# A graph stack on one core: the adjacency cast inside the loads that GpSimd issues, the other loads held back behind its pieces

## The chip, the cores and the metric

The kernel runs on one core of a Trainium2 chip. The metric is the device time of one execution in microseconds (us), and lower is better. The kernel before was timed three times; the median is 681.71 us, the runs lie between 681.45 and 682.27 us.

## What is computed

Four graph layers follow each other on the same 2048 x 256 features `x` and the same 2048 x 2048 adjacency matrix of zeros and ones. Each layer's result is added to its input and normalised by row.

```python
x = _layernorm(x + L0(x, adj))   # adj @ (x W) + b, 8 heads side by side
x = _layernorm(x + L1(x, adj))   # attention of 4 heads: adj is added to the scores, softmax over all rows
x = _layernorm(x + L2(x, adj))   # two convolutions: relu([x, adj @ x] W + b), with a residual
x = _layernorm(x + L3(x, adj))   # relu(adj_norm @ x @ W), adj_norm from the degrees of adj + 1
```

## The kernel before, in words

Names first. P is 128, T is 16 tiles of 128 rows, D is 256. `x` holds the features in float32, `xt` the transposed features as two half-precision parts: a high part, and a low part that holds what the high part lost. A product in this kernel is made of several TensorE products of such parts. R is 4, the number of PSUM banks that a stage uses in turn. The engines are written as separate programs that meet at semaphores, each in the order of its own code.

The adjacency comes as 16 pieces of 1 MiB in float32 (`adj_in`). Piece n covers two tiles of result rows, n // 2 * 2 and the next, and half of the tiles j that are summed over: the first eight for an even n, the last eight for an odd n. The matrix stays in SBUF as bf16 in `adj` for the whole program.

The program starts with the stage that the change is about, layer 0:

1. SyncE (SP) issues the loads of the transposed features (`XT_LOADS`, seven parts; the sixth holds tiles 8 to 11, the seventh 12 to 15), then four adjacency pieces in the order of `FIRST_LOADS` = 0, 2, 1, 3 into four float32 staging buffers, then the bias, `x` and further pieces. Every later piece waits until the piece four before it has been cast out of its staging buffer.
2. ScalarE (ACT) and VectorE (DVE) make the high parts of `xt` (`turned_hi`), DVE and GpSimd (POOL) the low parts (`turned_lo`, and the loop over `CHUNKS[5:]` on POOL, line 1186, five instructions of two tiles each for tiles 6 to 15). PE multiplies each tile with the weights (`project(0, t, ...)`, line 560, six matmuls for a tile), waiting for the tile's low part (`s_lo`). ACT and DVE take the products out of PSUM into `pset` (`take_p`, `take`).
3. PE sums over the graph (`agg_step`, lines 572 and 573, two matmuls for a pair of result tile and j). It starts with result tiles 0 to 3, piece by piece in the order of `FIRST_LOADS`, and waits for each piece's cast (`cast_done`). Then `rest` does tiles 4 to 15 one by one. Before tile t it waits for `s_sum` of tile t - 4, that is until DVE has added the product of tile t - 4 to `x` and so freed its bank; and for the casts of the tile's two pieces (`cast_ready`).
4. Behind PE, DVE sums (`first`, lines 811 and 812), takes statistics and normalises (line 796), ACT makes a high part (`gat_hi`, line 424). POOL adds the layer's bias to `x` ahead of the sum (`add_b0`, line 1191; DVE's `first` waits for it by `s_xb`), makes the inverse deviation (`inv_std`, lines 1197 and 1199) and the low part (`prep_lo`, line 1205). The casts stand between these: two on DVE (line 764), fourteen on ACT (line 416).
5. SP, after its last load, issues 16 DMA transposes (line 295), one for a normalised tile, two in flight at a time. The attention layer's projections on PE (lines 550 and 677) wait for them.

The attention layer follows from 120 us to about 450 us (lines 732 to 734 on PE), then layers 2 and 3, whose tiles also pass through DMA transposes. POOL issues 14 DMAs there that add `y` to `x` in the transfer (line 1249); they are the only DMAs that POOL issues in the kernel before.

## Time and profile before

| | |
|---|---|
| median of 3 timed runs | 681.71 us |
| the profiled execution, own time | 682.0 us |
| its span in the profile | 679.9 us |
| PE busy, share of the span | 671.5 us, 99% |
| DVE, ACT, POOL busy | 526.1, 387.3, 154.5 us |
| mean granted TensorE clock | 0.999 of full speed |

A busy PE means that matmuls are in the pipeline. One matmul of the graph sum is shown as 0.27 us long, though the next starts 0.11 us later; so a pause shorter than that does not show up as idle time and has to be read from the distance between starts. The execution's own time is 2.1 us longer than the span: what lies around the span.

### The profile page before, as it was taken

The numbers are of one execution on the slowest core, as the hardware profiler recorded it, in microseconds if no ns is written. First come the engines' busy times: TensorE is split into PE (matmuls) and PEld (weight loads), VectorE is DVE, ScalarE is ACT, GpSimd is POOL, SyncE is SP. The second block draws the span as 40 slices with busy tenths as digits, with TensorE's granted clock in tenths as the row PEclk, the third lists the DMA queues.
The fourth block names the chain that finished last, engine by engine and source line by source line (L and its number), as shares of the span: only waits on it lengthen the run. The fifth ranks groups of instructions, "written<-read, shape, count | busy, mean of one in ns | idle before, by whom it ended". The sixth has DMA issues, their size and how long they took to land.

```text
span 679.9 us, 14431 instructions
## 1 busy us (share of the span) xinstructions
PE 671.5 (99%) x5334; PEld 512.3 (75%) x5334; DVE 526.1 (77%) x991; ACT 387.3 (57%) x497; POOL 154.5 (23%) x252
## 2 busy tenths in 40 slices
PE   9999999999999999999999999999999999999996
PEld 7888644888888888888888888874444468886444
DVE  6267659998989989899897998999545435874785
ACT  6486358898889898898988979643101000222000
POOL 4366437401000010000101001564021102442222
PEclk9999999999999999999999999999999999999999
DMA  8999530003003030120301203013021110221011
GB/s 339 375 414 302 92 99 31 16 31 65 1 33 62 31 62 0 39 54 31 62 0 49 44 0 63 1 40 71 16 54 24 24 25 17 40 40 32 32 54 41
DMA packets 48297, 47.65 MB, mean 70 GB/s; under 512 B 36032, under 2 KB 42368, under 8 KB 46080
## 3 DMA queue, kind: packets, MB, share of 16 engines
q1 hardware_dynamic: 45664, 39.24, 18.9%
q0 software_dynamic: 2016, 7.34, 5.8%
q8 instruction: 26, 0.43, 0.3%
q10 hardware_dynamic: 576, 0.52, 0.2%
q14 instruction: 15, 0.12, 0.1%
HBM read 29.23 MB, written 2.13 MB: 46 GB/s over the span
## 4 chain that ended last, share of the span: by engine, by line
PE 83%; DMA 7%; DVE 4%; SPq 2%; ACT 1%; POOL 1%; issue 1%; POOLq 0%
PE ps L732 17%; PE ps L734 16%; PE ps L733 16%; PE ps L570 16%; PE ps L560 8%; DMA arena<-in_adj 4%; PE ps L573 4%; PE ps L572 4%; DMA ring_hl<-y 2%; SPq L295 2%; PE ps L677 2%; DVE arena L1026 1%; DMA ring_hl<-rho 1%; DVE ring_a L1070 1%; POOL rstd L1199 1%; ACT adj L416 1%
## 5 line engine op out<-in xcount | busy, mean ns | idle before, releaser
L734 PE MATMUL ps<-arena,ring_hl 128*128 (+1 forms) x1024 | 279.6, 273 | 0.0
L732 PE MATMUL ps<-arena,ring_hl 128*128 (+1 forms) x1024 | 278.8, 272 | 0.1
L733 PE MATMUL ps<-arena,ring_hl 128*128 (+1 forms) x1024 | 278.6, 272 | 0.0
L1070 DVE SCALAR_TENSOR_TENSOR ring_a<-rho,gam,ring_a 128x1024 f32<-128x1024 f32 x128 | 166.4, 1300 | 18.1 <-ACT ring_a L467 18.1
L1075 DVE TENSOR_TENSOR ring_hl<-ring_a,ring_hl 128x1024 f16<-128x1024 f32 x128 | 157.3, 1229 | 4.6 <-ACT ring_hl L481 4.6
L481 ACT ACTIVATE ring_hl<-ring_a 128x1024 f16<-128x1024 f32 x128 | 135.2, 1056 | 44.3 <-PE ps L734 27.6
L467 ACT ACTIVATE ring_a<-adj,shift 128x1024 f32<-128x1024 bf16 x128 | 145.7, 1139 | 0.0
L572 PE MATMUL ps<-arena,adj 128*128 128x257 f16 (+1 forms) x512 | 112.9, 273 | 0.7 <-ACT adj L416 0.7
L573 PE MATMUL ps<-arena,adj 128*128 128x256 f16 x512 | 112.9, 273 | 0.0
L570 PE MATMUL ps<-arena,adj 128*128 128x512 f16 x496 | 111.6, 379 | 0.0
L732 PEld LDWEIGHTS ps<-arena,ring_hl 128*128 128x128 f16 x1024 | 100.0, 98 | 12.9 <-DVE arena L1026 0.5
L733 PEld LDWEIGHTS ps<-arena,ring_hl 128*128 128x128 f16 x1024 | 99.1, 97 | 13.7
L734 PEld LDWEIGHTS ps<-arena,ring_hl 128*128 128x128 f16 x1024 | 99.5, 97 | 13.1
L570 PEld LDWEIGHTS ps<-arena,adj 128*128 128x128 bf16 x496 | 48.4, 98 | 57.8 <-DVE arena L817 0.3
L1249 POOL DMA_DIRECT2D x<-y x14 | 12.4, 882 | 273.6 <-ACT y L496 273.6
L379 ACT ACTIVATE arena<-ps 128x256 f16<-128x256 f32 (+1 forms) x48 | 18.4, 383 | 96.0 <-PE ps L560 96.0
L572 PEld LDWEIGHTS ps<-arena,adj 128*128 128x128 bf16 (+1 forms) x512 | 50.1, 98 | 7.5 <-issue 1.0
L573 PEld LDWEIGHTS ps<-arena,adj 128*128 128x128 bf16 (+1 forms) x512 | 50.1, 98 | 6.1
L1199 POOL TENSOR_TENSOR rstd<-veps,neghalf 128x1 f32<-128x1 f32 x64 | 42.4, 662 | 5.0
L677 PE MATMUL ps<-w,ring_hl 128*128 128x512 f16 x192 | 42.8, 379 | 0.0
L796 DVE TENSOR_SCALAR x<-total,mv,rstd 128x256 f32<-128x256 f32 x48 | 23.8, 497 | 21.9 <-POOL rstd L1199 21.5
L378 ACT ACTIVATE arena<-ps,dis2w 128x256 f32 x16 | 7.6, 474 | 55.5 <-PE ps L560 55.5
(112 smaller groups left out, 580.4 us busy)
## 6 DMA issues: line engine op xcount, KB each, us to landing
arena<-in_adj SPq DMA_DIRECT2D x16, 1024.0 KB, 11.6
x<-y POOLq DMA_DIRECT2D x14, 512.0 KB, 5.4
rho<-s_scratch SPq DMA_DIRECT2D x8, 512.0 KB, 3.8
x<-in_x SPq DMA_DIRECT2D x4, 512.0 KB, 13.8
out_x<-x SPq DMA_DIRECT2D x16, 128.0 KB, 1.7
arena<-in_x_turned SPq DMA_DIRECT2D x2, 512.0 KB, 5.6
arena<-in_L_gnn_W SPq DMA_DIRECT2D x1, 1024.0 KB, 11.5
arena<-in_L_gnn_a SPq DMA_DIRECT2D x1, 1024.0 KB, 13.5
```

The costliest lines, as they stand in the source:

```text
L467: nc.scalar.activation(ring_a[:, jt % SLOTS, :], adj[:, jt, q * CH:(q + 1) * CH], ACT.Exp, bias=shift[:, at(h, 1), jt]).then_inc(s_e, 1)
L481: nc.scalar.activation(ring_hl[:, jt % SLOTS, 0], ring_a[:, jt % SLOTS], ACT.Copy).then_inc(s_ah, 1)
L560: ins = nc.tensor.matmul(bank[:, 0:width], xpart(a, kk), w[:, b, kk, :], start=(n == 0), stop=(n == len(steps) - 1))
L570: ins = nc.tensor.matmul(ps[:, bank, :], lhs, pp[:, j, 0:2 * D], start=(j == 0), stop=(j == T - 1))
L572: nc.tensor.matmul(ps[:, bank, 0:width], lhs, pp[:, j, LOW:LOW + width], start=(j == 0), stop=False)
L573: ins = nc.tensor.matmul(ps[:, bank, 0:D], lhs, pp[:, j, 0:D], start=False, stop=(j == T - 1))
L677: ins = nc.tensor.matmul(ps[:, 2 * u + half, :], xtt[:, (a * K2 + kk) * P:(a * K2 + kk + 1) * P], w1[:, b, kk, half * 512:(half + 1) * 512 ...
L732: nc.tensor.matmul(acc, hi, v_hi, start=(jt == 0), stop=False)
L733: nc.tensor.matmul(ps[:, b, 0:D], hi, v_lo, start=False, stop=False)
L734: ins = nc.tensor.matmul(acc, lo, v_hi, start=False, stop=(jt == T - 1))
L1070: nc.vector.scalar_tensor_tensor(a, rho[:, q, :], gam[:, at(h, 1), jt], a, op0=ALU.max, op1=ALU.mult)\
L1075: nc.vector.tensor_sub(ring_hl[:, jt % SLOTS, 1], ring_a[:, jt % SLOTS], ring_hl[:, jt % SLOTS, 0])\
```

## The change

The adjacency is no longer staged and cast by ACT and DVE. POOL issues all 16 pieces itself, each as a DMA with a float32 source and a bf16 destination, so the transfer casts. Each piece has its own semaphore and PE waits for the transfer. The destination is laid out as result tile, then j (`adj` is now `[P, T, T, P]`), and the host lays the source out to match, so that a partition's 8 KB in memory fall on two runs in SBUF. SP keeps the other loads, and most of them now wait for a piece: the bias and the first two quarters of `x` for piece 0, the third for piece 5, the weights `w1` and the attention vectors for piece 8, the last quarter of `x` for piece 11. Tiles 2 and 3 are prepared singly on ACT and DVE instead of as a pair. Four DMA transposes may be in flight instead of two. Two conversions on DVE stand one step later, two bias loads on ACT move behind the stage, POOL's last four bias additions stand one step nearer to their use, and PE's loop over the last tiles of the first stage is unrolled.

```diff
-        CHUNKS = [(0, 1), (1, 2), (2, 4), (4, 5), (5, 6)] + [(t, t + 2) for t in range(6, T, 2)]
+        CHUNKS = [(t, t + 1) for t in range(6)] + [(t, t + 2) for t in range(6, T, 2)]
...
-            return s_tc[t % 2], 16 * ((k - 1) * T // 2 + t // 2 + 1)
+            return s_tc[t % TURNS], 16 * (((k - 1) * T + t) // TURNS + 1)
...
+            sp.wait_ge(ld_adj[FIRST_LOADS[0]], 16)
             sp.dma_start(bias0, b0_in.rearrange("(a n) -> a n", a=1).partition_broadcast(P)).then_inc(ld_b, 16)
...
             load_x(0)
-            load_adj(4)
-            load_adj(5)
             load_x(1)
-            load_adj(6)
-            load_adj(7)
+            sp.wait_ge(ld_adj[5], 16)
             load_x(2)
-            for n in range(8, 12):
-                load_adj(n)
-            sp.wait_ge(s_lo, T)
+            sp.wait_ge(ld_adj[8], 16)
             sp.dma_start(w1f, w1_in.rearrange("(k p) (h f) -> p k h f", p=P, h=H)).then_inc(ld_w1, 16)
...
-            load_adj(12)
+            sp.wait_ge(ld_adj[11], 16)
             load_x(3)
-            for n in range(13, NL):
-                load_adj(n)
...
-            for n in (1, 3, 4, 5, 6, 7):
-                cast_n(n)
-            CAST = cast_n
-            behind = {n - 5: [(CAST, n)] for n in range(8, NL)}
-            behind[7] = [(w1_hi, 0), (w1_hi, 1)] + behind[7]
-            behind[13] = [(was_hi,)]
+            behind = {7: [(w1_hi, 0), (w1_hi, 1)], 13: [(was_hi,)]}
...
-            casts_after = {11: 0, 15: 2}
-            turned_after = {3: 8, 5: 9}
+            turned_after = {4: 9, 6: 10}
...
-            pool.wait_ge(s_lo, CHUNKS[5][0])
-            for lo, hi in CHUNKS[5:]:
+            adj_n = adj_in.rearrange("c h p w -> (c h) p w")
+
+            def load_adj(n):
+                js = slice((n % 2) * JH, (n % 2 + 1) * JH)
+                nc.gpsimd.dma_start(adj[:, n // 2 * 2:n // 2 * 2 + 2, js, :],
+                                    adj_n[n].rearrange("p (i j c) -> p i j c", i=2, j=JH)).then_inc(ld_adj[n], 16)
+            pool.wait_ge(*xt_loaded(8))
+            load_adj(FIRST_LOADS[0])
+            pool.wait_ge(s_lo, CHUNKS[6][0])
+            later_loads = {1: FIRST_LOADS[1], 4: FIRST_LOADS[2]}
+            for n, (lo, hi) in enumerate(CHUNKS[6:]):
                 pool.wait_ge(s_hi, hi)
                 nc.gpsimd.tensor_sub(xt[:, lo:hi, D:2 * D], xts[:, lo:hi, :], xt[:, lo:hi, 0:D]).then_inc(s_lo, hi - lo)
+                if n in later_loads:
+                    load_adj(later_loads[n])
+            load_adj(FIRST_LOADS[3])
+            for n in range(4, NL):
+                load_adj(n)
             pool.wait_ge(ld_b, 16)
```

On POOL, the rows from the low parts of tiles 6 to 15 (written to `ring_hl`, which holds `xt`) to the first inverse deviations stood like this before; the eight rows that write `x` are `add_b0` for tiles 0 to 7:

```order
18 L1186 TENSOR_TENSOR ring_hl<-arena,ring_hl 128x2x256 [waits s_lo,s_hi,s_nh]
19 L1186 TENSOR_TENSOR ring_hl<-arena,ring_hl 128x2x256 [waits s_hi] x4
20 L1191 TENSOR_TENSOR x<-x,ring_a 128x256 [waits ld_x0,ld_b]
21 L1191 TENSOR_TENSOR x<-x,ring_a 128x256 [waits ld_x0] x3
22 L1191 TENSOR_TENSOR x<-x,ring_a 128x256 [waits ld_x1] x4
23 L1197 TENSOR_TENSOR veps<-mv,epsv 128x1 [waits s_aggr]
24 L1199 TENSOR_TENSOR rstd<-veps,neghalf 128x1 [waits s_ve]
```

The same stretch of POOL in the changed kernel, from the first load to the first inverse deviation:

```order
18 L1142 DMA adj<-in_adj 128x2x1024 [waits ld_xt5,s_nh]
19 L1150 TENSOR_TENSOR ring_hl<-arena,ring_hl 128x2x256 [waits s_hi,s_lo]
20 L1150 TENSOR_TENSOR ring_hl<-arena,ring_hl 128x2x256 [waits s_hi]
21 L1142 DMA adj<-in_adj 128x2x1024
22 L1150 TENSOR_TENSOR ring_hl<-arena,ring_hl 128x2x256 [waits s_hi] x3
23 L1142 DMA adj<-in_adj 128x2x1024 x14
24 L1160 TENSOR_TENSOR x<-x,ring_a 128x256 [waits ld_x0,ld_b]
25 L1160 TENSOR_TENSOR x<-x,ring_a 128x256 [waits ld_x0] x3
26 L1160 TENSOR_TENSOR x<-x,ring_a 128x256 [waits ld_x1] x4
27 L1166 TENSOR_TENSOR veps<-mv,epsv 128x1 [waits s_aggr]
28 L1168 TENSOR_TENSOR rstd<-veps,neghalf 128x1 [waits s_ve]
```

One DMA now stands ahead of the first low part, one between the second and the third, and fourteen between the last low part and the first bias addition.

On SP, the first rows of the kernel before, up to the first DMA transposes of the normalised tiles (`ring_hl<-y`), were:

```order
4 L259 DMA arena<-in_x_turned 128x1024 x2
5 L267 DMA arena<-in_adj 128x2048 x4
6 L270 DMA ring_a<-in_L_gnn_b 128x256
7 L273 DMA x<-in_x 128x4x256
...
14 L267 DMA arena<-in_adj 128x2048 [waits s_cast_act] x4
15 L284 DMA arena<-in_L_gnn_W 128x2x1024 [waits s_lo]
16 L285 DMA arena<-in_L_gnn_a 128x2048
17 L267 DMA arena<-in_adj 128x2048 [waits s_cast_act]
18 L273 DMA x<-in_x 128x4x256
19 L267 DMA arena<-in_adj 128x2048 [waits s_cast_act] x3
20 L295 DMA_TRANSPOSE ring_hl<-y 128x4x128 [waits s_lo] x2
```

And the same stretch of SP in the changed kernel:

```order
4 L245 DMA arena<-in_x_turned 128x1024 x2
5 L249 DMA ring_a<-in_L_gnn_b 128x256 [waits ld_adj0]
6 L252 DMA x<-in_x 128x4x256 x2
7 L252 DMA x<-in_x 128x4x256 [waits ld_adj5]
8 L258 DMA arena<-in_L_gnn_W 128x2x1024 [waits ld_adj8]
9 L259 DMA arena<-in_L_gnn_a 128x2048
10 L252 DMA x<-in_x 128x4x256 [waits ld_adj11]
11 L267 DMA_TRANSPOSE ring_hl<-y 128x4x128 [waits s_lo] x4
```

All adjacency loads have left SP, and the transposes follow the load that waits for piece 11 instead of the last piece.

## Rows read from the trace of the kernel before

**Rows 1.** The page: span, PE's busy time, the granted clock in 40 slices.
```profile
span 679.9 us, 14431 instructions
PE   671.5 (99%) x5334; PEld 512.3 (75%) x5334; DVE 526.1 (77%) x991; ACT 387.3 (57%) x497; POOL 154.5 (23%) x252
PEclk9999999999999999999999999999999999999999
```

**Rows 2.** Waits of PE over the whole span: total us, times, longest.
```profile
PE ps L652 <- POOL y L1164: 1.1, 1, 1.1
PE ps L572 <- ACT adj L416: 0.7, 1, 0.7
PE ps L560 <- DVE ring_hl L970: 0.5, 1, 0.5
```

**Rows 3.** PE's timeline at five places: start, us, line, shapes, count, idle before.
```profile
6.07 0.82 PE L560 MATMUL ps<-w,ring_hl 128*128 128x256 f16 x6
7.35 0.50 PE L560 MATMUL ps<-w,ring_hl 128*128 128x256 f16 x3 [0.47 <-DVE ring_hl L970]
...
10.74 1.31 PE L560 MATMUL ps<-w,ring_hl 128*128 128x256 f16 x8
...
16.81 0.27 PE L572 MATMUL ps<-arena,adj 128*128 128x257 f16 x1
16.92 0.27 PE L573 MATMUL ps<-arena,adj 128*128 128x256 f16 x1
...
60.53 0.27 PE L573 MATMUL ps<-arena,adj 128*128 128x256 f16 x1
61.52 0.28 PE L572 MATMUL ps<-arena,adj 128*128 128x257 f16 x1 [0.72 <-ACT adj L416]
...
84.17 0.65 PE L550 MATMUL ps<-was,ring_hl 128*128 128x16 f16 x8
```

**Rows 4.** The chain that ended last, around the last transposes.
```profile
82.08 2.43 DMA ring_hl<-rho
...
84.56 0.26 PE ps L550 x4
```

**Rows 5.** Timelines of ACT and DVE at the casts and conversions.
```profile
59.47 1.91 ACT L416 ACTIVATE adj<-arena 128x2048 bf16<-128x2048 f32 x1 [1.70 <-DMA arena<-in_adj]
8.49 0.62 ACT L399 ACTIVATE ring_hl<-arena 128x512 f16<-128x512 f32 x1
10.00 1.09 DVE L975 CAST ring_hl<-arena 128x512 f16<-128x512 f32 x1
11.68 0.71 DVE L975 CAST ring_hl<-arena 128x512 f16<-128x512 f32 x1
```

**Rows 6.** POOL's timeline: the first low part, and the bias additions.
```profile
8.53 1.16 POOL L1186 TENSOR_TENSOR ring_hl<-arena,ring_hl 128x512 f16<-128x512 f32 x1 [5.66 <-DVE ring_hl L970]
25.16 2.78 POOL L1191 TENSOR_TENSOR x<-x,ring_a 128x256 f32<-128x256 f32 x4 [10.65 <-DMA x<-in_x]
```

**Rows 7.** The five low parts on POOL: ns min/median/max.
```profile
L1186 POOL TENSOR_TENSOR ring_hl<-arena,ring_hl x5: 1148/1162/1342, 8.5 to 13.4; 128x512 f16<-128x512 f32 x5
```

**Rows 8.** The 14 DMAs that POOL issues: ns of one issue, us to landing.
```profile
L1249 POOL DMA_DIRECT2D x<-y x14: 852/862/1175, 161.1 to 415.1; - x14
DMA to landing us min/median/max: 4.5/5.4/7.5
```

**Rows 9.** DMA queues in 317 to 322, 160 to 172, 66 to 85 us.
```profile
q1 hardware_dynamic: 144, 0.52, 27.3%
...
q0 software_dynamic: 288, 1.05, 46.7%
...
q1 hardware_dynamic: 7379, 1.78, 52.8%
```

**Rows 10.** Stretches: us, busy by engine, clock, share of the DMA engines, GB/s.
```profile
17.00:30.00 13.00, 13.00 (x121) 11.60 (x120) 4.00 (x14) 6.12 (x4) 2.78 (x4) 1.00 0.95 363
30.00:50.00 20.00, 20.00 (x185) 17.86 (x183) 10.28 (x40) 14.83 (x14) 12.84 (x27) 1.00 1.03 414
50.00:66.00 16.00, 15.28 (x140) 13.41 (x138) 12.54 (x50) 11.07 (x11) 10.62 (x19) 1.00 1.02 333
```

**Rows 11.** DVE's timeline: the first sums of the graph stage.
```profile
27.38 0.16 DVE L811 COPY deg<-ps 128x1 f32<-128x1 f32 x1 [8.39 <-PE ps L573]
27.45 0.41 DVE L812 TENSOR_TENSOR total<-ps,x 128x256 f32<-128x256 f32 x1
```

**Rows 12.** The first eight transposes on SP's queue: ns of one issue, first and last start.
```profile
L295 SPq DMA_TRANSPOSE ring_hl<-y x8: 1189/1217/2113, 51.1 to 71.5; - x8
```

**Rows 13.** The page: the exponentials of the attention, ACT.
```profile
L467 ACT ACTIVATE ring_a<-adj,shift 128x1024 f32<-128x1024 bf16 x128 | 145.7, 1139 | 0.0
```

More of the change, by code:

```diff
@@ L60, in sem @@
             return ctx.enter_context(nc.semaphore(name))
-        adj = sb("adj", [P, T, N], BF16)
+        adj = sb("adj", [P, T, T, P], BF16)
         x = sb("x", [P, T, D], F32)
@@ L154, in graph_stack @@
         ld_xt = [sem(f"ld_xt{i}") for i in range(7)]
-        ld_adj = [sem(f"ld_adj{i}") for i in range(STAGES)]
+        ld_adj = [sem(f"ld_adj{i}") for i in range(NL)]
         ld_w0 = [sem(f"ld_w0{i}") for i in range(K2)]
@@ L168, in graph_stack @@
         s_warm = sem("s_warm")
-        s_tc = [sem(f"s_tc{i}") for i in range(2)]
+        s_tc = [sem(f"s_tc{i}") for i in range(TURNS)]
         s_accp, s_sump, s_vp = sem("s_accp"), sem("s_sump"), sem("s_vp")
@@ L220, in xt_loaded @@
             return ld_xt[next(n for n, (lo, hi) in enumerate(XT_LOADS) if lo <= t < hi)], 16
-        def cast_done(n):
-            if n < STAGES:
-                return (s_cast_act if n % 2 else s_cast), n // 2 + 1
-            return s_cast_act, n + 1 - STAGES // 2
-        def cast_of(n):
-            src = stage[:, n % STAGES, :].rearrange("p (j w) -> p j w", j=JH)
-            return adj[:, (n % 2) * JH:(n % 2 + 1) * JH, (n // 2) * LW:(n // 2 + 1) * LW], src
         PLACES = {3: {5: [0], 6: [1, 2], 7: [3, 4], 8: [5, 6], **{t: [t - 2] for t in range(9, T)}},
@@ L402, in _ @@
             w0_hi(1)
-            turned_hi(*CHUNKS[1])
-            turned_hi(*CHUNKS[2])
-            turned_after = {0: CHUNKS[3:5], 1: CHUNKS[5:6], 2: CHUNKS[6:7], 3: CHUNKS[7:8]}
+            for chunk in CHUNKS[1:4]:
+                turned_hi(*chunk)
+            turned_after = {0: CHUNKS[4:6], 1: CHUNKS[6:7], 2: CHUNKS[7:8], 3: CHUNKS[8:9]}
             for t in range(T):
@@ L409, in _ @@
                     turned_hi(*chunk)
-            for n, bi in enumerate((b1_in, b2_in)):
-                act.dma_start(b12[:, n, :], bi.rearrange("(a n) -> a n", a=1).partition_broadcast(P)).then_inc(ld_b12, 16)
-            def cast_n(n):
-                act.wait_ge(ld_adj[n % STAGES], (n // STAGES + 1) * 16)
-                nc.scalar.activation(*cast_of(n), ACT.Copy).then_inc(s_cast_act, 1)
             def was_hi():
@@ L434, in _ @@
                     step(*n)
+            for n, bi in enumerate((b1_in, b2_in)):
+                act.dma_start(b12[:, n, :], bi.rearrange("(a n) -> a n", a=1).partition_broadcast(P)).then_inc(ld_b12, 16)
             def rho_exp(h, q):
@@ L466, in exp_adj @@
                 act.wait_ge(s_shift, H)
-                nc.scalar.activation(ring_a[:, jt % SLOTS, :], adj[:, jt, q * CH:(q + 1) * CH], ACT.Exp,
+                nc.scalar.activation(ring_a[:, jt % SLOTS, :].rearrange("p (b c) -> p b c", b=BANKS), adj[:, q * BANKS:(q + 1) * BANKS, jt, :], ACT.Exp,
                                      bias=shift[:, at(h, 1), jt]).then_inc(s_e, 1)
@@ L567, in agg_step @@
                 pp = pset[k % 2]
-                lhs = adj[:, j, at(it * P, P)]
+                lhs = adj[:, at(it, 1), j, :].rearrange("p a c -> p (a c)")
                 if a in WHOLE:
@@ L610, in last_tile @@
                     for j in range(T):
-                        lhs = adj[:, j, (T - 1) * P:T * P]
+                        lhs = adj[:, T - 1, j, :]
                         for half, first in ((0, j == 0), (1, False)):
@@ L663, in _, with piece_loaded @@
                         agg_step(0, 0, it, it, j, j == T - 1)
-            def cast_ready(t, u, half):
-                pe.wait_ge(s_cast_act, t + (half + 1 - u % 2 - STAGES // 2))
-            rest(0, None, cast_ready)
+            def piece_loaded(t, u, half):
+                pe.wait_ge(ld_adj[t // 2 * 2 + half], 16)
+            rest(0, None, piece_loaded)
             def values_half(t, u, half):
@@ L980, in _ @@
                                                op0=ALU.mult, op1=ALU.subtract).then_inc(lo_made, 1)
-            turned_lo(*CHUNKS[1])
-            turned_lo(*CHUNKS[2])
-            casts_after = {11: 0, 15: 2}
-            turned_after = {3: 8, 5: 9}
+            for chunk in CHUNKS[1:4]:
+                turned_lo(*chunk)
+            turned_after = {4: 9, 6: 10}
             for t in range(T):
```

48 lines of the change are left out of this document (18 added, 30 removed).

## The prediction

> **What bounds the kernel now.** I read the page first: PE is busy for 671.5 of 679.9 us and its clock is granted in full in every slice [rows 1]. So the time can only fall where PE pauses, and the next view is PE's waits: three, 2.3 us together [rows 2]. The first, 1.1 us, is the start of the program, which the change leaves alone. As a busy PE hides short pauses, I then looked at PE's starts. Matmuls of 256 columns start 0.11 us apart (16.81 and 16.92) [rows 3]. Four places have larger distances before the attention starts:
>
> - Tile 2: the last of six matmuls that start at 6.07 starts at about 6.61, the next at 7.35. That is 0.74 where 0.11 is normal: 0.63 us lost, waiting for DVE's low part of the pair 2 and 3 [rows 2, 3].
> - Tile 8: eight matmuls from 10.74 span 1.31 us, where 7 x 0.11 + 0.27 = 1.03 would do: 0.28 us lost [rows 3].
> - Piece 13: 60.53 to 61.52 is 0.99, so 0.88 lost. ACT's cast of that piece starts at 59.47, having waited for the transfer, and takes 1.91 [rows 3, 5].
> - The last transposes: the chain shows a transpose of 2.43 us before the matmuls at 84.56; the group of eight began at 84.17 [rows 3, 4]. The four before the wait need under 0.1 us to start, so about 0.3 is lost.
>
> Together 2.1 us, 0.3% of 681.7, is all that can be won. Against it stands what POOL now does on this stage's path.
>
> **Gains, part by part.** Tiles 2 and 3 singly: tile 2 no longer waits for tile 3's part; PE can go on at about 6.75, so up to 0.6. DVE's two conversions one step later take the 1.09 us conversion [rows 5] out of the way of the bank that tile 8 needs: up to 0.28. Both only make PE reach tile 6 sooner, and what happens there is the next paragraph. The casts leave ACT and DVE; what PE sees of them is the 0.88 at piece 13. Four transposes in flight, started before the loads are through, remove the 0.3. ACT's other idle time, the unrolled loop and the moved bias loads are worth nothing on PE: PE streams beside them at its 0.11.
>
> **POOL's order, the first cost.** POOL executes in order. Ahead of the low part of tiles 6 and 7 stands the issue of piece 0, which waits for the transposed features of tiles 8 to 11. ACT converts these from 8.49 on [rows 5], so the issue starts at about 8.45. In the kernel before the low part started at 8.53 [rows 6], when DVE's part was ready. How long is an issue, c? The only ones in the trace are 14 accumulating DMAs of 128 runs, 0.862 us each (0.852 to 1.175) [rows 8]. The new ones have two runs per partition, 256 in all. If all the time went with the runs, c would be 1.72. So c lies between 0.86 and 1.72. I take 1.0, near the row, because partitions, queue and kind of operation are the same.
>
> With c = 0.86: issue 8.45 to 9.31, low parts 6/7 to 10.56 and 8/9 to 11.68 at 1.16 each [rows 7], issue to 12.56, low parts 10/11 to 13.99 (1.34, the longest of the five) and 12/13 to 15.25, 14/15 to 16.35. PE needs 1.31 us for two tiles (12 x 0.109). It starts tile 6 at 10.6 (9.98 before), tile 10 at 14.03, tile 14 at 16.65, and the graph sum at A = 17.96 instead of 16.81. So 1.15 us are lost, and the gains at tiles 2 and 8 are already inside that number. Each 0.1 on c adds 0.2. At c = 1.0: **+1.43**.
>
> The Trainium skill, page DMA: Bandwidth & Descriptors, section Anatomy of one DMA, calls descriptor generation "small, variable", with little incremental cost for many. By that c stays at the row's 0.86 and the whole sum comes out 0.8 us lower; no row here shows an issue of 256 runs.
>
> **POOL's order, the second cost.** Fourteen issues stand ahead of the first bias addition. They start at 16.35 + 2(c - 0.86) and take c + 0.04 each. Then one addition (0.70, from 2.78 for four) [rows 6] and DVE's two instructions (0.55) [rows 11]. Only then may PE start tile 4, which it reaches 14.03 after A (128 matmuls at 0.1096). The stall is 14 x (c + 0.04) + 1.25 - 14.03 - 1.61: nothing up to c = 0.99, and 14 us for each us above. At c = 1.0: **+0.1**. The next things on that chain, six more additions and the first inverse deviation for tile 6, stay about 1 us inside their 7.0 us.
>
> **DMA, the third cost.** From 30 to 50 us the engines were full at 414 GB/s [rows 10], 2.53 us for 1 MiB; I count 2.6. A plain packet of 4096 bytes costs 27.3% of 5 us for 0.52 MB, 2.7 us for a MiB; an accumulating one 46.7% of 12 us for 1.05 MB, 5.6 us, but that reads two sources [rows 9]. A cast reads one and writes half, so its price p is between 2.5 and 5.6, and I take 2.65. By about 18.7 pieces 0 and 2 and half of `x` are in. Twelve pieces and 3 MiB of other loads later, piece 13 lands at 18.7 + 12p + 7.8 = 58.3; PE wants it at A + 43.8 = 62.0. The casts are gone from that path, so the 0.88 is gone as well: **-0.88**, and **-0.3** for the transposes. But the transposes now start when piece 11 is in (about 53) instead of after all loads. Each costs the DMA engines 52.8% of 19 us over 14, 0.7 us [rows 9], and SP issues one every 1.3 us (1.217 and a gap) [rows 12]. Up to ten of them, 7 us of transfer, fall among pieces 12 to 15. Piece 15 would land at 18.7 + 14 x 2.65 + 7.8 + 7 = 70.6 against A + 50.9 = 69.1. That costs between 0 (if they fill gaps that the bulk packets leave) and 2 us; I take **+0.5**.
>
> **Sum.** +1.43 + 0.1 - 0.88 - 0.3 + 0.5 = +0.85 against the profiled execution's 682.0 (span 679.9 and 2.1 around it), which is 0.3 above the median. Against the median of 681.71 I forecast **682.6 us**, no change that a measurement tells. Such a measurement tells about 0.2%, 1.4 us, from nothing.
>
> **The rivals.**
>
> - *Issues dearer than the row.* At c = 1.1 the terms are 1.15 + 0.48 + 1.5 - 1.18 + 0.5 = +2.5, at 1.3 +5.7, at 1.72 +12.4. For it: twice the runs. Against it: nothing says the runs carry the 0.862. It decides from c = 1.03. A second way to the same place: DVE can hold POOL up. The same conversion took 1.09 us beside POOL's low part and 0.71 later [rows 5]. DVE was busy for 4.0 us between 17 and 30 [rows 10]; if all of that stopped the issues, c would seem 0.29 longer: +5.5. The Trainium skill states this rule, page SBUF — State Buffer, section SBUF: two separate sides: a DMA issued by GpSimd starves while DVE uses the port that they share. The pair 1.09 and 0.71 agrees that the two engines block each other; for a DMA issue no row here shows it. I count 30% for both.
> - *Cast packets slower than plain ones*, or the transposes costing their full 2 us. Piece 13 is late from p = 2.95. With the accumulating price of 5.6 the last piece lands at about 105 instead of 69, +36 us; at 3.2, piece 13 comes 2.9 late and the sum is about +4. 14%.
> - *Everything hidden.* POOL takes up the next instruction while descriptors are written (no row shows an instruction of POOL right behind an issue), or c is far below the row. Then the low parts keep up with PE, the sum starts at 16.3, and -0.5 - 0.88 - 0.3 = -1.7 gives 680.0. It is faster by over 0.2% only if c is under about 0.3 in effect and no piece is late. 20%.
> - *The forecast itself*, c up to 1.03 and pieces in time: 36%, its own range 681.3 to 683.0.
>
> **Range and chances.** The lower end 680.1 is the rival where all is hidden. The upper end is c = 1.4 with the full third cost or p = 3.3, both about +7: 688.7. Beyond it lie the dearest issues and the accumulating price, some 15%. Faster by over 0.2%: 20%. Within: 36%. Slower: 44%.
>
> **What would show it.** POOL's issue row: its mean ns against 0.86 to 1.72, and 16 of them, the last ending before about 31 us. The start of the graph sum on PE: 18.2, not 16.8 or 16.3. A wait of PE at tile 4, about 32 us, on DVE's sum (c above 1), where none was. No wait on ACT's line 416; a wait on a transfer near 60 to 68 us if p or the transposes are dear. The landing of pieces: 1 MiB every 2.6 us. The last transpose landed before 83 us. From 120 us on PE's rows should be the same as before, with the later start only. The prediction is wrong if POOL's issue does not delay the low parts, if PE's stretch from 30 to 73 us has other pauses than named, or if the attention's exponentials (line 467), which now read `adj` in runs of 128, get slower than their 1.14 us [rows 13] and leave their cover.

## The result, and the profile after

The changed kernel takes 690.06 us (median of four, 687.2 to 690.89), the kernel before 681.85 in the same session. The ratio is 1.0115, with a 95% interval of 1.0102 to 1.0127. The prediction was 682.6, with a range from 680.1 to 688.7. Of the 8.2 us by which the kernel got slower, its steps held 0.9. Where did the other 7.3 come from?

The page of the changed kernel, its first lines, answers to [rows 1]:

```profile
span 689.2 us, 14270 instructions
PE 673.8 (98%) x5334; PEld 512.2 (74%) x5334; DVE 522.7 (76%) x990; ACT 362.1 (53%) x484; POOL 166.4 (24%) x268
PEclk9999989999999999999999999999999999999999
```

The span is 9.3 us longer, and PE is busy for only 2.3 us more. So PE pauses, and in the sixth slice (86 to 103 us) the granted clock is below full, which no slice of the kernel before shows. PE's waits, the view of [rows 2] for the changed kernel:

```profile
PE ps L513 <- DVE was L961: 3.7, 1, 3.7
PE ps L523 <- POOL ring_hl L1150: 2.1, 1, 2.1
PE ps L523 <- DVE arena L739: 1.2, 2, 0.9
...
PE ps L535 <- DMA adj<-in_adj: 0.8, 1, 0.8
...
```

The longest is a wait for `was`, the low half of the attention's weight vectors, which DVE makes. The kernel before never waited there. PE's timeline of the changed kernel at the places of [rows 3]: start, us, line, shapes, count, and the idle time before.

```profile
6.95 2.79 PE L523 MATMUL ps<-w,ring_hl 128*128 128x256 f16 x24 [0.66 <-DVE ring_hl L928]
11.84 2.14 PE L523 MATMUL ps<-w,ring_hl 128*128 128x256 f16 x18 [2.10 <-POOL ring_hl L1150]
...
19.96 0.27 PE L535 MATMUL ps<-arena,adj 128*128 128x257 f16 x1
...
26.86 0.27 PE L536 MATMUL ps<-arena,adj 128*128 128x256 f16 x1
27.91 0.28 PE L535 MATMUL ps<-arena,adj 128*128 128x257 f16 x1 [0.78 <-DMA adj<-in_adj]
...
77.02 2.75 PE L640 MATMUL ps<-w,ring_hl 128*128 128x512 f16 x12
83.42 0.48 PE L513 MATMUL ps<-was,ring_hl 128*128 128x16 f16 x12 [3.65 <-DVE was L961]
83.77 2.72 PE L640 MATMUL ps<-w,ring_hl 128*128 128x512 f16 x6
86.65 2.72 PE L640 MATMUL ps<-w,ring_hl 128*128 128x512 f16 x6
89.53 1.48 PE L640 MATMUL ps<-w,ring_hl 128*128 128x512 f16 x6
```

Four losses can be read here. The graph sum starts at 19.96 instead of 16.81: 3.15 us. At piece 1 the starts are 26.86 and 27.91, 1.05 apart where 0.11 is normal: 0.94. The twelve matmuls from 77.02 start 0.215 apart, the last at 79.4; the next starts at 83.42: 3.8. And behind that pause six matmuls of 512 columns take 2.72 us, twice, where the same six take 1.48 afterwards: 2.5 us at half clock (1.2 in place of 2.4 GHz). Against them stand the gains that the prediction counted, 0.88 and 0.3. The sum is +9.2. It fits the span, which is 9.3 longer, and the start of the attention's own matmuls, 126.98 instead of 117.61. (The profiled executions' own times differ by 8.9, 690.89 against 682.0: what lies around the span is 0.4 shorter.)

One caution on the first of the four: in e7 and e8 below, kernels whose start is that of the kernel before, the graph sum began at 17.44 and 17.26. So up to 0.6 of the 3.15 may be what one execution differs from another.

Why is `was` late? The chain that ended last, of the changed kernel, from 23 to 84 us, tells it:

```profile
23.87 33.26 DMA adj<-in_adj
57.15 11.80 DMA x<-in_x
...
69.01 0.73 POOL x L1160
69.77 0.16 DVE deg L769
...
72.93 0.55 POOL rstd L1168
73.48 0.70 POOL x L1160
74.21 0.16 DVE deg L769
...
81.28 0.70 POOL x L1160
82.00 0.16 DVE deg L769
...
83.15 0.23 DVE was L961
83.42 0.48 PE ps L513 x12
```

The last quarter of `x` is issued when piece 11 has landed, at 57.15, and takes 11.80 us (in the kernel before it is issued at 43.8). POOL adds the bias to tile 12 of it, DVE sums tile 12 at 69.77. From there each tile goes round a loop: DVE's statistics, POOL's inverse deviation (L1168), POOL's addition for the next tile (L1160), DVE's next sum. A turn is 3.9 to 4.4 us, and PE makes a tile in 3.5, so nothing is caught up until `was` at 83.15. Two edits of the change meet here: the load waits for a piece, and the addition moved from two steps ahead to one.

The start, on POOL: the timeline of the changed kernel, against [rows 6], and then the row that groups the pieces' issues (ns min/median/max, first and last start), against [rows 8].

```profile
9.64 0.95 POOL L1142 DMA_DIRECT2D adj<-in_adj  x1 [6.78 <-DMA arena<-in_x_turned]
10.60 2.28 POOL L1150 TENSOR_TENSOR ring_hl<-arena,ring_hl 128x512 f16<-128x512 f32 x2
12.82 0.76 POOL L1142 DMA_DIRECT2D adj<-in_adj  x1
13.60 2.32 POOL L1150 TENSOR_TENSOR ring_hl<-arena,ring_hl 128x512 f16<-128x512 f32 x2
```
```profile
L1142 POOL DMA_DIRECT2D adj<-in_adj x16: 713/713/947, 9.6 to 26.7; - x16
```

An issue costs 0.713 us, less than the 0.862 of the accumulating ones and under the lower end that I gave. The Trainium skill, page DMA: Bandwidth & Descriptors, section Anatomy of one DMA, says that many descriptors can be emitted before their incremental cost shows. The row agrees: 256 runs took no longer than the 128 of [rows 8], though the two kinds of DMA differ. Fourteen in a row end at 27.4, in time for the bias additions. What is late is the first: 9.64, not the 8.45 of the prediction. The load that it waits for landed at 8.97; ACT, which waits for the same load, went on at 9.05. Why POOL began 0.6 later than ACT no run shows. The low part of tiles 6 and 7 behind it starts at 10.60 instead of 8.53. DVE's conversions are slow besides, on DVE's timeline, against 1.09 and 0.71 in [rows 5]:

```profile
11.12 2.69 DVE L933 CAST ring_hl<-arena 128x512 f16<-128x512 f32 x1
14.38 1.82 DVE L933 CAST ring_hl<-arena 128x512 f16<-128x512 f32 x1
```

The first ends at 13.81, 0.2 us behind POOL's second issue, the second at 16.20, 0.3 behind a low part. The Trainium skill, page SBUF — State Buffer, sections SBUF: two separate sides and Who interferes with whom, says that some of DVE's instructions, casts among them when their operands allow it, and GpSimd's lock each other out of a port that they share, whichever comes first holding it to its end. The two rows agree that far. But in the kernel before both conversions ran beside low parts as well (8.53 to 14.51) and took 1.09 and 0.71; why they take so much longer here no run shows. The sixteen issues don't show the other half of that rule, a starved DMA of GpSimd: their median is their minimum, and the second, beside the slow conversion, took 0.76.

### The profile page after: what moved, and what is told of

Its sections match the earlier page's. It is cut to its first block, busy times and chain, and to the rows that moved or that the text cites. A ratio compares the mean times of both kernels' runs of the same rounds, so it can differ in the third digit from the quotient of the medians.

```text
span 689.2 us, 14270 instructions
## 1 busy us (share of the span) xinstructions
PE 673.8 (98%) x5334; PEld 512.2 (74%) x5334; DVE 522.7 (76%) x990; ACT 362.1 (53%) x484; POOL 166.4 (24%) x268
## 4 chain that ended last, share of the span: by engine, by line
PE 87%; DMA 7%; DVE 3%; POOL 2%; issue 0%; SPq 0%; ACT 0%; POOLq 0%; DVEq 0%; ACTq 0%
PE ps L695 16%; PE ps L697 16%; PE ps L696 16%; PE ps L533 16%; PE ps L523 8%; PE ps L640 6%; DMA adj<-in_adj 5%; PE ps L535 4%; PE ps L536 4%; DMA x<-in_x 2%; POOL adj L1142 1%; DMA arena<-in_x_turned 1%; DVE ring_hl L933 1%; POOL x L1160 0%; POOL rstd L1168 0%
## 5 line engine op out<-in xcount | busy, mean ns | idle before, releaser
L533 PEld LDWEIGHTS ps<-arena,adj 128*128 128x128 bf16 x496 | 48.5, 98 | 57.7 <-DVE arena L775 0.3
L535 PEld LDWEIGHTS ps<-arena,adj 128*128 128x128 bf16 x512 | 50.1, 98 | 7.5 <-DMA adj<-in_adj 1.1
L536 PEld LDWEIGHTS ps<-arena,adj 128*128 128x128 bf16 x512 | 50.1, 98 | 6.1
L640 PE MATMUL ps<-w,ring_hl 128*128 128x512 f16 x192 | 45.4, 394 | 0.0
L1168 POOL TENSOR_TENSOR rstd<-veps,neghalf 128x1 f32<-128x1 f32 x64 | 43.4, 678 | 5.0
L1166 POOL TENSOR_TENSOR veps<-mv,epsv 128x1 f32<-128x1 f32 x64 | 16.1, 252 | 108.2 <-DVE mv L807 82.4
## 6 DMA issues: line engine op xcount, KB each, us to landing
arena<-in_L_gnn_a SPq DMA_DIRECT2D x1, 1024.0 KB, 12.8
```

The lines of the kernel that those rows point to most:

```text
L533: ins = nc.tensor.matmul(ps[:, bank, :], lhs, pp[:, j, 0:2 * D], start=(j == 0), stop=(j == T - 1))
L535: nc.tensor.matmul(ps[:, bank, 0:width], lhs, pp[:, j, LOW:LOW + width], start=(j == 0), stop=False)
L536: ins = nc.tensor.matmul(ps[:, bank, 0:D], lhs, pp[:, j, 0:D], start=False, stop=(j == T - 1))
L640: ins = nc.tensor.matmul(ps[:, 2 * u + half, :], xtt[:, (a * K2 + kk) * P:(a * K2 + kk + 1) * P], w1[:, b, kk, half * 512:(half + 1) * 512 ...
```

## The experiments

Each ratio is to the kernel before, run on the same chip in the same session.

**The late quarter of x, the additions, and both (first session; before 681.32 us).** The theory then: the late quarter alone makes `was` late.

```
e1:  load_x(2)
    +load_x(3)
     sp.wait_ge(ld_adj[8], 16)
     ... w1 and the attention's vectors ...
    -sp.wait_ge(ld_adj[11], 16)
    -load_x(3)
e2: -if 3 * R <= t + 1 < T:
    -    add_b0(t + 1)          (between inv_std and prep_lo)
    -if 2 * R <= t + 2 < 3 * R:
    +if 2 * R <= t + 2 < T:
         add_b0(t + 2)          (after prep_lo)
e3:  e1 and e2
```

> Only the last quarter of x is loaded earlier: right behind the third quarter instead of behind piece 11. Theory (the late quarter sets GpSimd's bias addition for tile 12, then DVE's sums of tiles 12 to 15, then the attention's weights, for which TensorE waits 3.7 us at 79.4 and after which its clock is halved for some 10 us): the quarter lands before 57 us, DVE takes tile 12 at about 67 instead of 69.8, then one tile every 3.9 us since the addition still stands only one step ahead; the weights are ready at about 79.9 instead of 83.4, TensorE waits under 1 us, the clock stays up: 685.5 us (684.5 to 686.5). Rival 1 (the clock falls whatever that wait is, for example from the earlier pauses): wait gone, clock still at half for 10 us: about 687.5. Rival 2 (the wait comes from the position of the bias additions alone): no change, 690. Rival 3 (the pieces are what matters, and half a MiB ahead of piece 6 delays them): PE waits on transfers between 40 and 70 us, above 688.

> Only the bias additions of tiles 12 to 15 go back to two steps ahead; the quarter of x stays late (68.9 us). Theory (late quarter and short lead act together): tile 12's addition still ends at 69.7, but tiles 13 to 15 follow at GpSimd's pace of 2.2 to 3 us (71.9, 74.9, 77.0) instead of 3.9 to 4.4, so the weights are ready at about 78.3, before TensorE needs them at 79.4: wait and half clock gone, 684.3 us (683.5 to 685.5). Rival (the late quarter alone decides, and GpSimd now waits for it with the inverse deviation of tile 11 behind it): the same 690 or later, up to 692.

> Both: the quarter of x early and the additions two steps ahead. Theory: no wait of TensorE at 79.4 and no half clock; what is left over the kernel before is the later start of the graph sum (3.15) and the piece at 26.9 (0.95) less the gains at piece 13 and at the transposes: 684.2 us (683.4 to 685.0), and the graph sum still ends at about 76.8 instead of 73.6. Rival (clock independent of the wait): 687.

Measured: e1 692.59 us (ratio 1.016, 1.0144 to 1.0175), e2 688.1 (1.0103, 1.0088 to 1.0119), e3 689.65 (1.0122, 1.0106 to 1.0137). All three miss. e1 is slower than the changed kernel beyond both intervals: the vectors landed at 63.1, DVE waited 5.5 us for them, and PE's wait for `was` grew to 6.2 us. In e2 that wait was 3.0 us and the clock stayed up, where the theory had no wait. (The expectation of e1 speaks of some 10 us at half clock in the changed kernel; its trace shows 6, from 83.4 to 89.5.) e3 has both mends and is no faster than the changed kernel (1.0115). PE's wait for `was` in e3 is again 3.7 us. The chain that ended last, of e3:

```profile
21.87 21.14 DMA adj<-in_adj
43.03 0.38 SPq L259
43.45 17.93 DMA arena<-in_L_gnn_a
...
61.52 0.43 DVE ring_a L920
...
82.60 0.23 DVE was L960
```

The quarter is in time, but half a MiB ahead of them has pushed the attention's vectors (`in_L_gnn_a`) to 61.4 us; in the changed kernel they landed at 57.3, 12.8 us after their issue at 44.5. DVE's products of the weights wait for them (4.9 us), tiles 10 to 15 queue behind the products, and again nothing is caught up. So the theory was too narrow. The step that it lacked: DVE's turn is about as long as PE's tile even with the additions two ahead (in e2 DVE starts tiles 12 to 15 at 69.1, 73.0, 76.1 and 79.5), so any load that is late on this path, the quarter of `x` or the vectors, is late to the end.

**More of the start, and it costs (same session).** e4 is e3 with the first piece's issue behind the first low part, the second's behind the last, and DVE's conversions one take earlier.

```
    -load_adj(FIRST_LOADS[0])           (ahead of the low parts)
    -later_loads = {1: FIRST_LOADS[1], 4: FIRST_LOADS[2]}
    +later_loads = {0: FIRST_LOADS[0]}
    ... behind the low parts ...
    -load_adj(FIRST_LOADS[3])
    +for n in FIRST_LOADS[1:]:
    +    load_adj(n)
    -turned_after = {4: 9, 6: 10}
    +turned_after = {3: 9, 5: 10}
```

> The kernel with both, and besides the first piece issued behind the first low part instead of ahead of it, the second behind the last low part, and DVE's conversions of tiles 12 to 15 one take earlier, as in the kernel before. Theory (two issues of 0.95 and 0.76 us and the late conversion hold up the low parts): tile 6 is projected 0.95 us earlier and the graph sum starts at about 18.2 instead of 19.96; but the second piece is issued at about 15.5 and its landing (5.4 us later, about 21) is what the sum then meets at 21.6: 682.6 us (681.8 to 684.2). Rival (the later landing of the transposed features sets the start, not the issues): no change against the kernel with both, 684.2.

Measured: 690.2 us (1.0127, 1.0107 to 1.0148), a miss. Two of its waits of PE say why:

```profile
PE ps L534 <- DMA adj<-in_adj: 3.2, 1, 3.2
PE ps L522 <- DVE arena L738: 2.4, 1, 2.4
```

The sum started at 19.36, 0.7 earlier than in e3, and then stood 3.2 us for the second piece, piece 2. PE's timeline of e4 behind that wait:

```profile
26.25 0.40 PE L534 MATMUL ps<-arena,adj 128*128 128x257 f16 x1 [3.22 <-DMA adj<-in_adj]
26.44 0.42 PE L535 MATMUL ps<-arena,adj 128*128 128x256 f16 x1
```

The two start 0.19 us apart and the next ones 0.21, where 0.11 is normal: here too the clock had fallen. The second piece must be issued early, not late.

**All loads early (second session; before 681.46 us).**

```
e5: -sp.wait_ge(ld_adj[5], 16)   +sp.wait_ge(ld_adj[4], 16)     load_x(2)
    -sp.wait_ge(ld_adj[8], 16)   +sp.wait_ge(ld_adj[5], 16)     w1, vectors
    -sp.wait_ge(ld_adj[11], 16)  +sp.wait_ge(ld_adj[7], 16)     load_x(3)
e6:  e5, and the additions two steps ahead (as e2)
```

> Of the changed kernel only the order of SP's loads moves: the third quarter of x waits for piece 4 instead of 5, the attention's weights (w1 and the broadcast vectors) for piece 5 instead of 8, the last quarter of x for piece 7 instead of 11. What the runs so far showed: whichever of these loads is late (57 and 69 us in the changed kernel, 61 us for the vectors where the quarter of x went first), DVE and GpSimd go on from it at 3.5 to 3.9 us per tile, as fast as TensorE delivers tiles, so the delay is carried to the attention's weights. Theory: with both in before about 58 us, DVE takes tile 12 at 66.8 and tile 15 at 78.5 (3.9 a tile), the weights come at 79.6, TensorE waits under 0.5 us, no half clock: 684.3 us (683.5 to 685.3). Rival 1: the pieces then are late (3 MiB more among pieces 4 to 11) and TensorE waits for them: above 686. Rival 2: the additions one step ahead alone keep the wait at over 1 us: 686 to 687. Rival 3 (something that the two loads don't touch): 690.

> The same loads, and the bias additions of tiles 12 to 15 two steps ahead as in the kernel before. Theory: DVE follows TensorE at 3.5 us a tile, the weights are ready at 78.3, no wait at 79.4: 683.9 us (683 to 684.8); what stays over the kernel before is the start of the graph sum, 19.96 or so against 16.81. Rival (the position of the additions is worth nothing with loads in time): the same as with the loads alone.

Measured: e5 686.91 us (1.0079, 1.0065 to 1.0092), e6 685.87 (1.0066, 1.0052 to 1.008). PE's waits in e6:

```profile
PE ps L523 <- POOL ring_hl L1150: 2.0, 1, 2.0
...
PE ps L535 <- DMA adj<-in_adj: 0.7, 1, 0.7
PE ps L513 <- DMA ring_hl<-rho: 0.2, 1, 0.2
```

The wait for `was` is gone, and with it the half clock. From the changed kernel to e6 the ratio falls by 0.49%, 3.3 us. The two profiled executions differ by more, 6.5 us (690.89 and 684.43), about the 3.8 and 2.5 that are gone; but the one is the slowest of its kernel's runs and the other the fastest. In e5, with the additions still one step ahead, a wait of 1.6 us for `was` is left. Its median is 1.0 above e6's; the intervals overlap, so of the place of the additions the wait is shown and the time is not. Both kernels missed, 2 us and more above what I expected. e5 came out where its rivals 1 and 2 had it: it waits 2.5 us for pieces 1 and 9, and 1.6 for `was`. What e6 lacks is open: its timed runs lie up to 2.2 us above the execution that was profiled, which was the fastest.

**The cause put into the kernel before (same session).** Nothing of the change, only the last quarter of `x` behind the last piece.

```
    -load_adj(12)
    -load_x(3)
    -for n in range(13, NL):
    +for n in range(12, NL):
         load_adj(n)
    +sp.wait_ge(ld_adj[3], 64)
    +load_x(3)
```

> The kernel before, with the last quarter of x issued only when the last piece has landed (about 64.6 us), so that it lands at about 68 instead of 57, near the 68.9 of the changed kernel; nothing else is changed. Theory: DVE takes tile 12 at about 69 instead of 63.6 and cannot catch up, the weights come at about 80 instead of 75.4, TensorE waits about 4 us at 76.2 and its clock is at half afterwards: 688.5 us (686 to 690). Rival 1 (the clock does not follow from the wait): 685.5. Rival 2 (DVE catches up, since it has idle time in this stretch): under 683.

Measured: 687.58 us (1.0085, 1.0071 to 1.0098), as expected. It is 6.1 us slower by a load that is not on any list of PE's waits. The chain that ended last, PE's longest wait and PE's timeline, all of e7:

```profile
64.34 3.56 DMA x<-in_x
...
67.96 0.72 POOL x L1191
```
```profile
PE ps L550 <- DVE was L1006: 4.9, 1, 4.9
```
```profile
81.79 2.72 PE L677 MATMUL ps<-w,ring_hl 128*128 128x512 f16 x6
...
86.80 1.46 PE L677 MATMUL ps<-w,ring_hl 128*128 128x512 f16 x6
```

The same wait and the same half clock come, with casts on ACT, plain loads and the additions two ahead. This settles that the quarter's lateness is enough. DVE took tile 12 at 68.72 instead of 63.55. It had idle time (12.6 us before its sums in the kernel before, 8.4 of them ahead of the first) and yet did not catch up.

**Parts of the change alone, in the kernel before.** e8: four transposes in flight (`TURNS = 4` and four semaphores). e10 (third session, before 682.35 us): tiles 2 and 3 singly, DVE's conversions one take later.

```
e10: -CHUNKS = [(0, 1), (1, 2), (2, 4), (4, 5), (5, 6)] + [(t, t + 2) for t in range(6, T, 2)]
     +CHUNKS = [(t, t + 1) for t in range(6)] + [(t, t + 2) for t in range(6, T, 2)]
     -turned_after = {3: 8, 5: 9}
     +turned_after = {3: 9, 5: 10}
```

> One part of the change alone: the kernel before with four transposes in flight (four semaphores) in place of two; loads and casts as before. Theory (a wait of about 0.3 us for the last transposes is all they cost): 681.4 us, 0 to 0.4 under the kernel before. Rival (four in flight disturb each other or the other transfers): 0.5 us or more slower.

> One part of the change alone: the kernel before, with tiles 2 and 3 converted singly and DVE's conversions of tiles 12 to 15 one take later, as in the change. Theory (0.6 us are lost at tile 2 and 0.3 at tile 8, and POOL's low parts of tiles 6 to 15, 1.16 each, keep up): 681.0 us, 0.2 to 0.8 under the kernel before. Rival (the low parts of tiles 6 and 7, which start at the same 8.5, take over the wait): no difference, 681.5.

Measured: e8 681.58 us (1.0003, 0.9994 to 1.0012), e10 681.87 (1.0000, 0.9990 to 1.0011). Neither does anything that can be measured there; the 0.2 to 0.8 us that I expected of e10 did not come. In e10 a wait of 0.4 us for POOL's low part stands where none stood before, as its rival said.

**The first issues early (third session).** e9 is e6 with this edit; e12 is the changed kernel with this edit alone; e11 is the changed kernel with the last quarter of `x` issued by POOL behind piece 10.

```
    -pool.wait_ge(*xt_loaded(8))
    +pool.wait_ge(*xt_loaded(4))
     load_adj(FIRST_LOADS[0])
    +load_adj(FIRST_LOADS[1])
     ... the low parts ...
    -later_loads = {1: FIRST_LOADS[1], 4: FIRST_LOADS[2]}
    +later_loads = {4: FIRST_LOADS[2]}
```

> The kernel with the earlier loads and the additions two steps ahead, and now GpSimd issues the first two pieces together as soon as the transposed features of tiles 4 and 5 are in (about 7.0 us), ahead of all low parts; before, the first waited for tiles 8 to 11 (9.5 us) and stood in front of the low part of tiles 6 and 7, and the second stood between two low parts. Theory (these two issues, 0.95 and 0.76 us, and what piles up behind them make the graph sum start at 19 to 20 us instead of 16.8): the low parts start at about 8.7 instead of 10.4, TensorE's wait of 2.0 us at tile 6 goes, the graph sum starts at about 17.2, and all after it moves up: 682.5 us (681.5 to 683.8), 3.4 under the kernel it comes from. Rival (the issues are not what holds the start, but DVE's conversions of tiles 12 to 15, 2.7 us each where they took 1.1): at most 1 us is won, 685.

> The changed kernel with only the two first issues early (as above), all loads and additions as in the change. Theory (two separate losses, about 3 us at the start and about 6 at the weights): the start comes back, about 17.2 for the graph sum, but the last quarter of x still waits for piece 11 and lands at 66 or later, so the weights are ready at about 80.5 while TensorE wants them at 76.6: a wait of 3 to 4 us stays, and in part eats the gain: 687.5 us (686 to 689). Rival (the late start delays all, loads too, and is the only cause): 683.

> The changed kernel with one thing else: the last quarter of x is issued by GpSimd in its own queue behind piece 10, not by SP after piece 11 has landed. Theory (the quarter takes 11.8 us because it waits for piece 11 and then shares the engines with the pieces that are queued already, a small packet for each large one; in the pieces' own queue it costs only its 1.3 us): it lands at about 53 us instead of 68.9, DVE takes tile 12 at 66.8 and follows at 3.9 us a tile, TensorE waits under 1 us for the attention's weights: 686.3 us (685.3 to 687.5). Rival (the attention's vectors at 57.3 us alone carry the delay): DVE's tile 12 still at over 68, no gain.

Measured: e9 683.12 us (1.0020, 1.0008 to 1.0031), e12 686.42 (1.0070, 1.0049 to 1.0092), e11 686.17 (1.0056, 1.0037 to 1.0074). All three lie in the ranges given. e9 gives back 0.46% against e6, 3.1 us. Its trace explains only a part: the sum starts at 18.15 instead of 19.87, 1.7 earlier, and of that 1.1 goes into a longer wait for piece 9 (1.8 instead of 0.7); the profiled executions differ by 1.0. e12 returns 0.45%, and a wait of 2.4 us for `was` stays. It does not part the two losses cleanly: the sum starts 1.6 us earlier (18.38), but the pieces come earlier too, the quarter of `x` is issued at 53.45 instead of 57.15, and the wait for `was` is 1.3 shorter than in the changed kernel. In e11 the quarter was issued at 23.75 and landed at 54.1. It took 30.4 us, longer than the 11.80, since it stood behind nine pieces that had not landed; but it landed 15 us earlier than in the changed kernel, and the wait for `was` fell to 1.2.

**What is left (fourth and fifth session; before 681.91 and 681.78 us).** e13 shifts e9's loads again (`x`'s third quarter behind piece 3, the weights behind 6, the last quarter behind 8). e14 is e13 with DVE's two conversions on ACT, e15 is e14 with two transposes in flight. e16 is the changed kernel with the first issues early, the additions two ahead and the last quarter right behind the weights, which stay behind piece 8; e17 is e16 with the conversions on ACT.

```
e14: -turned_after = {0: CHUNKS[4:6], ... 3: CHUNKS[8:9]}                     (ACT)
     +turned_after = {0: CHUNKS[4:6], ... 3: CHUNKS[8:9], 4: CHUNKS[9:10], 5: CHUNKS[10:11]}
     -turned_after = {4: 9, 6: 10}                                            (DVE)
     +turned_after = {}
e16: -sp.wait_ge(ld_adj[11], 16)
      load_x(3)
```

> The last kernel with the first two issues early, and SP's loads shifted once more: the third quarter of x one piece earlier (behind piece 3), the attention's weights and the last quarter of x one piece later (behind pieces 6 and 8). Theory (at 47.8 TensorE waits 1.8 us for piece 7, since 2.5 MiB of other loads share the engines with pieces 5 to 8): the wait at piece 7 falls under 0.5 us; the quarter of x lands by 61, still ahead of DVE's tile 12 at about 64: 681.6 us (680.9 to 682.8). Rival (the sum is fixed: another piece, or the weights, is late in its place): no gain, 683.1.

> The same, and the conversions of tiles 12 to 15, which DVE did in 2.7 us each (1.1 in the kernel before) with TensorE's banks waiting behind it, go to ACT, which has nothing else to do since it casts no more. Theory (they cost TensorE 0.96 and 0.27 at 12.2 and 14.5 us): the graph sum starts at about 17.2 instead of 18.2: 680.7 us (680 to 681.9), 0.9 under the run above. Rival (ACT, which also takes half of the banks, passes the same delay on; or the sum then waits for piece 1): under 0.3 us of gain.

> As the run above, with two transposes in flight instead of four, as in the kernel before. Theory (the number in flight is worth nothing as long as the last transpose lands before TensorE wants it, at about 83 us): within 0.4 us of the run above. Rival 1 (with two, the last transposes come late, as they did by 0.3 us in the kernel before): 0.3 to 1 us slower. Rival 2 (four crowd out the last pieces): faster.

> The changed kernel with three edits: the first two issues early, the additions two steps ahead, and the last quarter of x issued right behind the attention's weights (after piece 8) instead of after piece 11; the third quarter and the weights stay where the change has them. Theory (pieces 5 to 8 are late only when the weights' 2 MiB stand beside them, and from piece 9 on there is slack of 3 us): no wait of TensorE for a piece, weights in at 53 us, the quarter at 57 to 58, ahead of DVE's tile 12 at 63.9, no wait for the attention's weights: 681.8 us (681 to 683). Rival (the sum of transfers is too large wherever they stand): a later piece or the last transposes are waited for, 683 to 684.5.

> The same, and the conversions of tiles 12 to 15 on ACT. Theory (the graph sum starts 1 us earlier, at 17, and the pieces have the slack for it): 681.0 us (680.2 to 682.3), level with or below the kernel before. Rival (a second earlier in the sum only means a second's wait for a piece or a transpose, as in the run with the later loads): equal to the run above, within 0.3.

Measured: e13 684.3 us (1.0039, 1.0024 to 1.0053), e14 684.4 (1.0040, 1.0026 to 1.0054), e15 685.11 (1.0052, 1.0039 to 1.0065), e16 682.69 (1.0017, 1.0004 to 1.0030), e17 684.83 (1.0047, 1.0033 to 1.0061). PE's timeline of e13 where it waits for a piece, then PE's waits for transfers of e15 and of e16:

```profile
49.85 0.28 PE L535 MATMUL ps<-arena,adj 128*128 128x257 f16 x1 [1.43 <-DMA adj<-in_adj]
```
```profile
PE ps L513 <- DMA ring_hl<-rho: 2.3, 2, 1.5
```
```profile
PE ps L512 <- DMA ring_hl<-rho: 1.1, 1, 1.1
```

e13 missed: it still waits 1.4 us for a piece, only 0.4 less than e9. My expectation named the wrong one. By PE's count the wait at 48 to 50 us is in the middle of tile 8, which is piece 9: in e9 that piece landed at 49.8, piece 7 already at 39.5. So an edit meant for piece 7 moved the weights' issue from 33.3 to 36.6 us, nearer to the piece that is waited for. e14, e15 and e17 missed as well; e15 came out where its first rival had it. In e16 no piece is waited for, as expected, but the last transposes are, 1.1 us, as its rival said. The conversions on ACT do what was expected of them in the trace (the sum starts at 17.29 in e14 against 18.46 in e13, at 16.88 in e17 against 18.22), and the profiled executions are 1.3 and 1.0 us faster for it; but the medians are not. e14's is level with e13's, and e17's is 2.1 us above e16's, beyond both intervals, which neither its theory nor its rival (level within 0.3) had. e15 shows 2.3 us of waiting for transposes with two in flight, 0.6 in e14 with four; the medians differ by 0.7, and the intervals overlap. That an earlier start of PE is mostly a longer wait for some transfer, as the rivals had it, shows in e9 against e6; the trace of e17 does not show it. No version of the changed kernel beats the kernel before; e16 comes nearest, 0.17% behind it.

## Why the prediction was wrong

**The step that failed** is in the third cost: "Twelve pieces and 3 MiB of other loads later, piece 13 lands". It priced the other loads by their bytes, as time taken from the pieces, and asked only when the pieces are wanted. It never asked when `x`'s last quarter and the attention's vectors land, who waits for them, and what stands behind. The additions' move to one step ahead was not priced either: of the additions the text said only that they "stay about 1 us inside" at tile 6, and nothing of tiles 12 to 15. In its place the runs showed: late loads and the additions together cost 3.3 us (the changed kernel to e6), 3.8 us of wait and 2.5 of half clock in the profiled execution, and the quarter's lateness alone costs 6.1 in the kernel before (e7). The pieces that gate these loads were late as well: piece 11 landed at 57.2 where the prediction had about 53, and piece 13 at 62.5 where it had 58.3. Piece 1 had landed only at 27.8.

**The start was mis-sized.** +1.43 was predicted, and in the trace it is +3.15; 1.7 us of the start come back when the first issues move (e9), 1.6 also without the other mends (e12), and the times fall by 0.46% and 0.45%. The mechanism, an issue ahead of the low parts, was right. Its size was not c: c came out at 0.713, by which the same sum gives +0.9. The first issue began 1.2 us later than I took from ACT's conversion, 0.5 of it because the load landed later and 0.6 behind ACT's start on the same load, and DVE's conversions took 2.69 and 1.82 instead of 1.09 and 0.71. That the conversions cost in the trace is shown by e14 and e17 (1.2 and 1.3 us of earlier start); no gain in the medians came of it.

**Right were:** the 14 issues (last end 27.4, before 31; no stall at tile 4); and nearly the price of a piece. From 30 to 50 us the pieces' queue shows this, of the changed kernel:

```profile
q0 software_dynamic: 1849, 3.56, 94.7%
```

3.56 MB written are 7.12 MB or 6.8 MiB read; 94.7% of 20 us makes 2.79 us a MiB, where 2.65 was taken. Right as well: the 0.88 at piece 13 is gone, and the exponentials take 1.139 us as in [rows 13]. Too much was hoped of tiles 2 and 3 (up to 0.6) and of the transposes (0.3): neither is worth anything in the kernel before (e10, e8), and in the changed kernel PE still stands 0.66 us for DVE's low part, at 6.95. The 0.94 at piece 1 was in no term.

**Slips in sums and readings.** At c = 1.0 the second cost is 14.56 + 1.25 - 14.03 - 1.61 = 0.17, not 0.1. With c at 0.86 the whole sum is 0.4 lower, not 0.8. And c = 1.4 with the full third cost gives 2.23 + 5.77 - 1.18 + 2 = +8.8, not +7. Worked out rightly, the upper end would have been 690.5 and the measured time inside it, but by luck: c was 0.713, and the time went elsewhere. The pair 1.09 and 0.71 said less than I took from it, since the second conversion too ran beside POOL's low parts.

**The rivals:** dear issues and dear packets did not come; the slower side was reached by none of those named. The text's own list of what would make it wrong named "other pauses than named" up to 73 us, and the pause came at 79.4.

**Open:** the last 0.2% of e9 and e16, and why e17 is slower than e16. The timed runs of the kernels with cast pieces scatter more (e14 682.55 to 686.56, e17 681.66 to 686.15, the kernel before 680.71 to 682.55 in the session of e17), so the traces of e6, e14 and e17, taken in their fastest executions, don't show what their slower ones wait for. In that of e17 the attention's matmuls start at 117.89, almost as in the kernel before (117.61).

## What to carry to other kernels

When loads change their order or their queue, list for each load, not only for the one that is changed, when it lands, who reads it, and whether the stage behind has speed to spare; a loop over two engines whose turn is as long as PE's tile carries any late input to its end, however idle its engines look. A load beside a deep queue of others should be issued before the queue fills, or take an early enough place in that queue. And a mend is tried together with its neighbours: the first one here (e1) made the kernel slower, because it handed the lateness to the next load.

## What the runs showed of the hardware

**A small load beside a deep queue.** The quarter of `x`, 512 KB, took 3.56 us from issue to landing in e7, where all pieces had landed and only transposes followed it, and 11.80 in the changed kernel, with pieces queued (11.69 in e2, 11.66 in e12). The queues there, from 57.5 to 68.5 us, and the load's row:

```profile
q0 software_dynamic: 766, 1.46, 70.5%
q1 hardware_dynamic: 1137, 0.67, 50.9%
...
x<-in_x SPq DMA_DIRECT2D x1, 512.0 KB, 11.8
```

The Trainium skill, page DMA: Bandwidth & Descriptors, section SWDGE vs HWDGE vs iDMA, says that GpSimd's and SP's DMAs feed different queues inside each DMA engine and that the engine goes round between them. The trace agrees so far as both queues move at once.

**The clock after a pause.** The granted clock was 1.00, which is 2.4 GHz, in the stretch of matmuls ahead of each of these pauses. After waits of 2.4 (e12), 3.2 (e4, at piece 2), 3.7 (the changed kernel, e3), 4.9 (e7) and 6.2 us (e1) it was 0.50, which is 1.2 GHz, for some 2 to 6 us (in e12 only from 1.7 us after the wait on). After 1.6 us (e5), 2.2 (e4, for `was`) and 3.0 us (e2) it stayed up. So the price of a pause was up to 2.5 us above its length; and as 2.4 us brought the clock down and 3.0 did not, the length of a wait alone does not tell whether it falls.
